# The last expert stage of a six-stage decoder as one program, its routing spread over the expert units

## The reference, cut to what matters

```python
x = x + _L1_ffn_ref(_layernorm(x, axis=-1), ...)

def _L1_ffn_ref(X, routing_W, expert_bias, sW1, sb1, sW2, sb2, rW1, rb1, rW2, rb2):
    shared = jax.nn.silu(X @ sW1 + sb1) @ sW2 + sb2            # 256 -> 128 -> 256
    logits = jnp.einsum('btd,ed->bte', X, routing_W) + expert_bias
    activation = jnp.sqrt(jax.nn.softplus(logits))
    top_vals, top_idx = jax.lax.top_k(activation, 2)
    combine = jnp.sum(jax.nn.one_hot(top_idx, 8) * top_vals[..., None], axis=-2)
    hdn = jax.nn.silu(jnp.einsum('nd,edh->enh', Xf, rW1) + rb1[:, None, :])
    y = jnp.einsum('enh,ehd->end', hdn, rW2) + rb2[:, None, :]
    return shared + jnp.einsum('ne,end->nd', cf, y)            # cf: combine, by token
```

## Time and profile before

| | us |
|---|---|
| median of 3 runs | 1856.62 (1855.23 to 1857.04) |
| the profiled execution, its own time | 1860.18 |
| its span in the trace | 1858.5 |
| the last stage: first instruction to end of the span | 1540.87 to 1858.5 |
| its `up` of the first unit begins | 1632.52 |
| its last product ends | about 1849.7 |

### The profile page before, as it was taken

The page is one execution under the profiler, slowest core; times in us unless marked ns, Lnnn a source line. Parts: engine busy times, 40 slices in busy tenths (PEclk is TensorE's granted clock), DMA queues, the critical chain, the costliest instruction groups (busy, mean ns, idle before and its releaser), DMA issues. The chain is left out here.

```text
span 1858.5 us, 33579 instructions
## 1 busy us (share of the span) xinstructions
PE 1334.2 (72%) x12235; PEld 1026.7 (55%) x12235; DVE 1092.5 (59%) x1991; ACT 759.4 (41%) x1278; POOL 734.9 (40%) x628
## 2 busy tenths in 40 slices
PE   3777648788773329999999277844788872299997
PEld 1555425566652218888888277522556542256665
DVE  4777645777665655555555562374777746744443
ACT  1222335656545643433334140132576671234433
POOL 1110147989873363444444110061577893000000
PEclk9787768788765559999999655555887875599999
DMA  3000066654514421222122520007523210000000
GB/s 138 1 0 0 18 135 110 111 95 70 86 19 139 158 80 56 60 64 64 58 64 58 201 107 2 0 0 149 123 53 70 53 19 0 1 12 12 23 23 23
DMA packets 83949, 114.07 MB, mean 61 GB/s; under 512 B 11620, under 2 KB 68070, under 8 KB 81384
## 3 DMA queue, kind: packets, MB, share of 16 engines
q1 hardware_dynamic: 76328, 91.78, 21.6%
q0 software_dynamic: 7488, 20.46, 3.7%
HBM read 72.98 MB, written 31.20 MB: 56 GB/s over the span
## 5 line engine op out<-in xcount | busy, mean ns | idle before, releaser
L2756 POOL TENSOR_TENSOR q_pl<-q_ex,q_ph 128x512 f16<-128x512 f32 x128 | 147.0, 1161 | 44.4 <-ACT q_ph L2710 44.0
L1776 POOL TENSOR_TENSOR r_siml<-r_sim,r_simh 128x512 f16<-128x512 f32 x128 | 146.2, 1161 | 21.3 <-ACT r_simh L1680 20.9
L1089 POOL DMA_INDIRECT expert_results<-mt_yout,m_deliver x78 | 77.4, 993 | 171.4 <-ACT mt_yout L1177 159.4
L2559 DVE TENSOR_REDUCE q_mx<-q_pS 128x4 f32<-128x512 f32 x128 | 86.5, 685 | 76.1 <-PE q_pS L2487 75.5
L1538 DVE TENSOR_TENSOR r_sim<-r_pS,r_causal 128x512 f32<-128x512 f32 x128 | 86.5, 682 | 60.3 <-PE r_pS L1452 56.5
L1122 PE MATMUL mt_pU<-mt_xh,m_w 128*128 128x256 f16 x624 | 116.2, 274 | 1.5 <-DVE mt_xl L1198 1.5
L1680 ACT ACTIVATE r_simh<-r_sim 128x512 f16<-128x512 f32 x128 | 79.9, 628 | 90.2 <-DVE r_sim L1538 85.6
L1122 PE MATMUL mt_pV<-mt_xh,m_w 128*128 128x256 f16 x624 | 115.2, 273 | 0.0
L1133 PE MATMUL mt_pY<-m_w,mt_hh 128*128 x624 | 106.5, 272 | 10.8 <-DVE mt_hl L1212 10.7
L2704 ACT ACTIVATE q_ex<-q_pE 128x512 f32<-128x512 f32 x128 | 76.6, 599 | 67.4 <-PE q_pE L2508 44.3
L2978 DVE TENSOR_TENSOR s_hc<-s_h,s_pC 128x512 f32<-128x512 f32 x64 | 44.0, 688 | 100.8 <-ACT s_h L2947 100.8
(11 more groups left out here) (503 smaller groups left out, 4144.3 us busy)
## 6 DMA issues: line engine op xcount, KB each, us to landing
ahead<-in_L_ffn_W SPq DMA_DIRECT2D x12, 1024.0 KB, 5.0
r_kstack<-k_bounce SPq DMA_DIRECT2D x48, 128.0 KB, 4.7
r_qstack<-q_bounce SPq DMA_DIRECT2D x48, 128.0 KB, 5.9
q_Q<-m_bounce SPq DMA_DIRECT2D x24, 256.0 KB
X<-in_x SPq DMA_DIRECT2D x4, 1024.0 KB, 7.9
r_ctx<-in_ctxT SPq DMA_DIRECT2D x8, 512.0 KB, 5.6
k_bounce<-r_ksplit SPq DMA_DIRECT2D x32, 128.0 KB, 2.6
q_bounce<-r_qsplit SPq DMA_DIRECT2D x32, 128.0 KB, 2.4
```

The lines of the kernel that those rows point to most:

```text
L1089: pool.indirect_dma_start(results[:, :], bass.IndirectOffsetOnAxis(ap=deliver[:, at:at + 1], axis=0), yout[n % 2][:, a, :], None).then_inc ...
L1776: pool.tensor_tensor(siml[n % RING][:, :], sim[n % SIMS][:, :], simh[n % RING][:, :], ALU.subtract)\
L2559: dve.tensor_reduce(mx[:, at:at + UNIT], pS[n % 2][:, :, :], AX, ALU.max).then_inc(s["taken"], 1)
L2756: pool.tensor_tensor(pl[n % RING][:, :], ex[n % 3][:, :], ph[n % RING][:, :], ALU.subtract)\
```

## The change

The blocks 1 to 4 become one program. Every engine's stream is written out over steps k from -22 to 73, where step k holds unit k (k = 9 g + j) and whatever of the routing is due there. The routing is done for a **pair** of groups (8 sequences, tiles of 128 x 64) at fixed steps ahead of the pair's first unit, 18 q; for pair 0 all these steps lie ahead of unit 0. `Router`, `choose_two`, `Shares` and `constants` go. So do the products `pC`: the shares are turned on TensorE, copied by ACT, written to DRAM and read back into 128 partitions at once (16 KB each, 2 MB a group, two buffers). The bias of the second layer is one product a sequence at the last expert in place of two at the first. `take` works in two halves, and the next group's first `down` waits for each half alone. Normalization moves from DVE to ACT.

The diff, cut ("..." marks what is left out):

```diff
+    PAIR = 2 * GB
+    UNITS = NG * N
+    PAIR_UNITS = 2 * N
+    FIRST = -22
+    def scheduled(k, at):
+        q, rest = divmod(k - at, PAIR_UNITS)
+        return q if rest == 0 and 0 <= q < NG // 2 else None
+
+    def later_for_first(k, at, first):
+        if k == first:
+            return 0
+        q = scheduled(k, at)
+        return q if q else None
...
+        spread_share = [c.sb(f"spread_share{i}", [P, E, GT]) for i in range(2)]
...
             @block.sync
...
+                def keep_shares(q):
+                    sync.wait_ge(s["share_out"], q + 1)
+                    sync.dma_start(A["shares"][q], share_out[:, :]).then_inc(s["share_kept"], 16)
+                    sync.wait_ge(s["share_kept"], 16 * (q + 1))
+                def load_shares(g):
+                    if g >= 2:
+                        sync.wait_ge(hc_done, N * (g - 1))
+                    rows_of_group = A["shares"][g // 2][g % 2 * GB * E:(g % 2 + 1) * GB * E, :]
+                    sync.dma_start(flat(spread_share[g % 2][:]), rows_of_group.rearrange("a t -> (a t)")
+                                   .partition_broadcast(P)).then_inc(spread_in[g % 2], 16)
...
+                for q in range(NG // 2):
+                    if q > 0:
+                        store(2 * q - 2)
+                    keep_shares(q)
+                    load_shares(2 * q)
+                    load_shares(2 * q + 1)
+                    if q > 0:
+                        store(2 * q - 1)
             @block.gpsimd
...
+                for q in range(NG // 2):
+                    invert(q)
             @block.tensor
...
+                for k in range(FIRST, UNITS + 2):
+                    if k == 0:
+                        pe.wait_ge(split.low_done, 2)
+                    if k == 2:
+                        pe.wait_ge(split.low_done, 4)
+                        pe.wait_ge(s["b2_rows"], 1)
+                    if 0 <= k < UNITS:
+                        up(k)
+                    q = later_for_first(k, -4, 2)
+                    if q is not None:
+                        turn_shares(q)
+                    for at, run in ((-16, lambda q: transpose(2 * q)),
+                                    (-13, lambda q: (weigh(2 * q), transpose(2 * q + 1))),
+                                    (-10, lambda q: weigh(2 * q + 1))):
...
+                    for a in range(2):
+                        q = scheduled(k, 3 + a)
+                        if q is not None:
+                            turn_parts(2 * q + a)
+                    if k >= 2:
+                        down(k - 2)
             @block.scalar
...
+                split.high(act)
+                act.activation(ident16[:, :], ident[:, :], ACT.Copy).then_inc(s["made"], 1)
+                act.wait_ge(s["tables_in"], 16 * TABLES)
+                for k in range(FIRST, UNITS + 1):
+                    if 0 <= k < UNITS:
+                        silu(k)
+                    if k >= 1:
+                        high(k - 1)
+                    for at, run in ((-18, lambda q: norm(2 * q, 0)), (-17, lambda q: norm(2 * q, 2)),
+                                    (-16, lambda q: rows_high(2 * q)),
+                                    (-15, lambda q: norm(2 * q + 1, 0)), (-14, lambda q: norm(2 * q + 1, 2)),
+                                    (-13, lambda q: rows_high(2 * q + 1)), (-9, exponent), (-8, logarithm), (-7, root),
+                                    (-4, take_shares), (3, lambda q: take_parts(2 * q)),
+                                    (4, lambda q: take_parts(2 * q + 1))):
...
             @block.vector
...
+                    if j == 0:
+                        dve.tensor_copy(hc[k % RING][:, :], h[k % RING][:, :]).then_inc(hc_done, 1)
+                    else:
+                        dve.wait_ge(spread_in[g % 2], 16 * (g // 2 + 1))
+                        dve.tensor_tensor(hc[k % RING][:, :], h[k % RING][:, :], spread_share[g % 2][:, j - 1, :],
+                                          ALU.mult).then_inc(hc_done, 1)
...
+                for k in range(FIRST, UNITS + 2):
+                    if 0 <= k < UNITS:
+                        weigh(k)
+                    if 1 <= k <= UNITS:
+                        low(k - 1)
+                    if k > N and k % N == 1:
+                        take(k // N - 1)
+                    for at, run in ((-22, lambda q: stats(q, 0)), (-21, lambda q: stats(q, 1)), (-20, combine),
+                                    (-19, negate), (-15, lambda q: rows_low(2 * q)), (-12, lambda q: rows_low(2 * q + 1)),
+                                    (-10, take_logits), (-9, add_one), (-8, softplus), (-7, choose_first),
+                                    (-6, choose_second), (-5, cut)):
...
+                    if k == -20:
+                        split.low(dve, [0])
+                    if k == -19:
+                        split.low(dve, [1])
+                    if k == -10:
+                        dve.wait_ge(s["tables_in"], 16 * TABLES)
+                        split.low(dve, [2])
+                    if k == -5:
+                        split.low(dve, [3])
+                        stack_b2()
```

More of the change, by code:

```diff
@@ L499, in _ @@
                 main(NG - 1, False, None)
[L502 to L568, removed]
@@ L2876, in run @@
-        def run(eng, group, tail):
-            group(0, True)
-            with eng.Fori(1, NG) as g:
-                group(g, False)
-            tail()
+        stat = r.sb("stat", [P, B, 6])
+        apart, apart2, both, dev, devs, mean, ve, rstd, shift = (
+            r.sb(n, [P, B]) for n in "apart apart2 both dev devs mean ve rstd shift".split())
+        rows = [r.sb(f"rows{i}", [P, GB, D]) for i in range(2)]
+        lg, ab, ex, u, um, ln, lnt, quo, l1p, l1px, pos, sp, act_, picked, val, first, masked, second, chosen = (
+            r.sb(n, [P, PAIR, E]) for n in "lg ab ex u um ln lnt quo l1p l1px pos sp act picked val first masked second "
+                                           "chosen".split())
@@ L2928, in tail, with transpose @@
-                def tail():
-                    down(NG - 1, N - 2)
-                    down(NG - 1, N - 1)
-                run(pe, group, tail)
+                def transpose(g):
+                    pe.wait_ge(s["xn"], GB * (g + 1))
+                    if g > 0:
+                        pe.wait_ge(s["xl"], g)
+                    for dc in range(DC):
+                        for b in range(GB):
+                            last = pe.transpose(turn[:, dc, b * S:(b + 1) * S], rows[g % 2][:, b, dc * P:(dc + 1) * P],
+                                                ident[:, :])
+                    last.then_inc(s["turned"], 1)
@@ L2933, in _, with norm @@
             @block.scalar
             def _(act):
-                def high(g, j):
-                    k = g * N + j
+                def norm(g, b0):
+                    act.wait_ge(s["shifted"], g // 2 + 1)
+                    if g >= 2:
+                        act.wait_ge(s["turned"], g - 1)
+                    for b in range(g * GB + b0, g * GB + b0 + 2):
+                        act.activation(rows[g % 2][:, b % GB, :], X[:, b, :], ACT.Identity, scale=rstd[:, b:b + 1],
+                                       bias=shift[:, b:b + 1]).then_inc(s["xn"], 1)
@@ L2937, in high, with silu @@
+                def silu(k):
+                    act.wait_ge(u_done, k + 1)
+                    if k >= RING:
+                        act.wait_ge(hc_done, k - RING + 1)
+                    act.activation(h[k % RING][:, :], pU[k % RING][:, :], ACT.Silu, bias=b1[:, k % N:k % N + 1],
+                                   scale=1.0 / SCALE).then_inc(h_done, 1)
+                def high(k):
                     act.wait_ge(hc_done, k + 1)
-                    if not (starts(g, 0) and j < RING):
+                    if k >= RING:
@@ L2953, in _ @@
-                nc.scalar.preload_act_table(ACT.Silu)
-                run(act, group, lambda: high(NG - 1, N - 1))
+                    act.activation(hh[k % RING][:, :], hc[k % RING][:, :], ACT.Copy).then_inc(hh_done, 1)
+                split.high(act)
[12 more added lines that the diff above has]
+                                    (4, lambda q: take_parts(2 * q + 1))):
+                        q = scheduled(k, at)
+                        if q is not None:
+                            run(q)
```

458 lines of the change are left out of this document (237 added, 221 removed).

## The result

The changed kernel took 1810.36 us (median of 4, 1809.59 to 1816.52), the kernel before 1855.92 beside it (4 runs, 1853.77 to 1857.04): a ratio of 0.9763 [0.974, 0.9787], some 45 us faster. The forecast was 1809, its range 1793 to 1826. The profiled execution took 1809.59 us with a span of 1807.9; the one of before took 1860.18 with 1858.5.

A forecast was written before the change was run, and what follows sets the result against it. TensorE was taken to bound the expert loop, with 91.6 us ahead of it. First `down` 1585.0 + work 202.1 + tables 13.2 + clock 2 = 1802.3; with tail 8.7, span 1811.0, 47.5 less: median 1809, range 1793 to 1826.

The forecast's parts named there:

- What bounds it: Last stage: expert loop bound by TensorE; 91.6 us stand ahead of it, nearly all that work moving under the loop.
- The head: Stage start to first `down`: pair 0's routing in line, then write 2.4 and load 7.6 us; first `down` at 1585.0.
- The wait for `b2_rows`: In the head, TensorE's third `up` waits for `b2_rows`, with the turn of the shares behind it; copied by 1573.6.
- The loop: First `down` to last product: TensorE's work 202.1 us, table stalls 13.2, clock 2.
- bias: In the loop: 32 products of 256 columns, each a twelfth of 1.31 us, 3.5 us in all.
- tables: Exp, Ln, Sqrt between Silus in three units a pair: stalls 4.4 us a pair, 13.2 for three; bounds 0 and 26.
- clock: In the loop, three places with stalls could each see a lower-clock window: 2 us taken, bounds 0 and 10.
- `take` at nothing: TensorE's wait for the sum with the input, 4.7 us over seven groups before, costed at nothing beside an `up`.
- Rival 1: In the loop, table switches are mostly hidden and it runs at TensorE's price: 1796, chance 0.17.
- Rival 2: In the loop, stalls double as VectorE's pieces overrun and the clock falls: 1809 + 13, up to 1825, chance 0.17.
- Rivals 3 and 4: Share loads: late at 12 to 15 us, 1817 to 1829, chance 0.08; or about 21, slower than before, chance 0.04.
- Rival 5: In the loop's table units, a switch costs 2.66 us, drain included: 25 us more, 1834, chance 0.02.

The follow-up runs named there:

- a4_seventh: Changed kernel with the first product of every `up` done twice, 72 more products of 512 columns: 1819.74 us, ratio 0.9824 to the kernel before.
- a3_early: Changed kernel with pair 0's turn of the shares ahead of the third `up` and the `b2_rows` wait moved to the first bias product: 1802.82 us.
- c1_rows128: Changed kernel with the bias product's operands taken at 128 rows, the added share rows zero: 1794.42 us, ratio 0.9722 to the kernel before.
- c2_grouped: Changed kernel with a group's four bias products, still of 64 rows, issued one after another: 1796.21 us, ratio 0.9725 to the kernel before.
- a1_copy: Changed kernel with the routing's Exp, Ln and Sqrt replaced by copies, so no table loads; routing values differ: 1796.46 us, ratio 0.9702.
- b1_whole: Changed kernel with the sum of a group's result and the input taken in one piece instead of two: 1802.06 us, ratio 0.9758.
- c4_twice: Changed kernel with a second, unread 2 MB load of the same shares ahead of the group's own in pairs 1 to 3: 1800.51 us.

## Why the prediction was right

The number is within 1.4 us of the median, but not every term is, and part of the closeness is luck. The span was forecast at 1811.0 and came out at 1807.9; 2.9 of these 3.1 us are the stage's earlier start, which has no term in the record. By the steps of the record:

- **What bounds it**: right. The loop is TensorE's (`a4_seventh`), the gain is the head, and it is 48.2 us of the 50.6.
- **The head**: 44.1 us from the stage's start forecast, 43.4 measured. Its steps, from the same start: share there at 26.7 (27.0), `b2_rows` at 29.2 (29.7), copy of the turned share at 32.7 (33.1), write 2.4 (1.8), load 7.6 (7.1 from issue to VectorE's start). One price was off: POOL's power on 128 x 8 takes 1.64 us, not the 1.0 of 128 x 4. The size of an operand of a few columns matters there; on VectorE it doesn't. Not all of that lateness stayed: the router's products ended at 18.2 where 17.6 was forecast, but the share was only 0.3 late. The head is 0.7 shorter than forecast because the write and the load were 1.1 us cheaper together.
- **The wait for `b2_rows`** holds the head as the record said, and taking the turn out from behind it gave 3.1 us (`a3_early`).
- **The loop**: 217.3 forecast to the end of its last product, 217.6 measured, by errors that cancel; this agreement is luck. The *bias* was priced at a twelfth of an `up`, 3.5 us for 32. Its spacing is 0.32, so 10.3, and the two runs on it give 6.6 (`c1_rows128`) and, with 24 of the 32 steps gone, 5.0 (`c2_grouped`) of the difference back. That is the mis-sized term: the record took the time of a product with 128 rows for one with 64 rows between others of 128. The *tables* were priced at 13.2 us and cost 9.1 (`a1_copy`): the record had four stalls a pair, 1.7, 0.8, 1.45 and 0.5 us, and the trace has three, 0.5, 0.6 and 1.4, with none behind `choose_second`. The *clock* was put at 2 us and cost nothing: granted 0.99 over the stretch, 1.00 in each of its windows behind 1587. (The start at the lower clock had a term of its own, 1.5 us.) Together 18.7 taken for these three, 19.4 found.
- **`take` at nothing**: 1.4 us measured, in the three table units alone, which is where the record had put it. Elsewhere it costs nothing; in one piece it would cost 0.24 us in each of two other groups (`b1_whole`).
- **Rival 1** (1796) fails on the 9.1 us. **Rival 2** fails: without the tables one wait of 0.8 us is all that is left. **Rivals 3 and 4** fail on the load: 2 MB in 7.0 us, even with the pair's other load issued 0.4 us behind it, which landed after 11.5. VectorE's wait for it stands once, at the start. `c4_twice` adds that even 11.6 to 12.8 us a load cost 1.4 in all three pairs. **Rival 5**: the Trainium skill, "ScalarE: Activation LUTs", section "What ACT_TABLE_LOAD costs", has about 1380 ns of drain beside the 1283 ns of the load. This trace agrees with the load and shows no drain: 0.01 us between the copy's end and the load in the lines above, 1.28 us in the load, 0.02 from its end to Exp; two switches and Exp take 2.9 us from the copy's end to the next Silu.

What the record's own signs said: first `down` near 1585 (1581.4, of which 2.9 is the stage's earlier start), first Silu near 1575 (1572.4, 2.6 earlier), 18 loads in the loop (18), 4 us of idle TensorE beside each triple (2.4), units of 2.61 us elsewhere, clock at 1.00. None of its signs looked at the bias, where the mis-sized term was.

## What to carry to other kernels

When a product is added to a row of others, look at the shape of its weights as well as its columns: padded with zeros to the same rows it was three times cheaper here, and where that can't be done, put all of them in a row. Work that is hidden under a bound engine costs what it puts in the *order* of the small engines' queues: a table load, a sum or a wait standing in front of the next unit's piece; a longer lag cures only what flows through the lagging buffers. And a total that agrees proves no term: only stage-relative times and one run per term told that 6.8 us too little and 4.1 and 2 too much had met.

## What was unexpected of the hardware

- A step between matmuls with 64 and with 128 rows of weights costs TensorE 0.10 us each way at the full clock, shown as issue time ahead of the weight load.
- POOL's power took 1.64 us on 128 x 8 and 1.0 on 128 x 4, while VectorE's small instructions took 0.17 on both.
- One DRAM row of 16 KB read by 128 partitions ran no slower for its size than the 1 MB load (5.0 us): 2 MB in 7.0 us. Of two such loads issued 0.4 us apart on one queue the first still took 7.0 and the second 11.5.
- The same code ahead of the stage ended anywhere within 14 us over 13 profiled executions, most of it from one set of runs to another, and still within 2.3 to 4.8 us inside a set. Head and stretch of one kernel, profiled twice, repeated to 0.1 us.
